# Turning the feed-forward's rounded values in fp32 instead of bf16, in a one-core transformer block

## The reference, cut to what matters

```
def act_quant(x):
    scale = 127.0 / jnp.clip(jnp.max(jnp.abs(x), axis=-1, keepdims=True), 1e-05)
    return jnp.clip(jnp.round(x * scale), -128, 127) / scale
...
h = bit_linear(x, w1)                      # 128 -> 512
h = depthwise_conv1d(h.transpose(0, 2, 1), conv_w, conv_b)
h = jax.nn.silu(h.transpose(0, 2, 1))
return bit_linear(h, w2)                   # act_quant(h), 512 -> 128, w2 in {-1, 0, 1} times a scale
```

## Time and profile before

| what | before |
|---|---|
| median of 3 runs | 264.71 us (264.69 to 265.05) |
| the profiled execution | 264.35 us |
| its span, first to last instruction | 262.4 us |
| TensorE busy | 254.0 us (97%) |
| VectorE busy | 217.1 us (83%) |
| ScalarE busy | 192.2 us (73%) |
| GpSimd busy | 31.1 us (12%) |

### The profile page before, as it was taken

The page is one execution under the profiler, slowest core; times in us unless marked ns, Lnnn a source line. Parts: engine busy times, 40 slices in busy tenths (PEclk is TensorE's granted clock), DMA queues, the critical chain, the costliest instruction groups (busy, mean ns, idle before and its releaser), DMA issues.

```text
span 262.4 us, 5607 instructions
## 1 busy us (share of the span) xinstructions
PE 254.0 (97%) x1869; PEld 189.2 (72%) x1869; DVE 217.1 (83%) x534; ACT 192.2 (73%) x463; POOL 31.1 (12%) x53
## 2 busy tenths in 40 slices
PE   7899999999999999999999999989999999999996
PEld 3568779779779878868787788767657565575675
DVE  5599979866766698998999787889899999899861
ACT  1689887788658678697899966179998699834551
POOL 3000002000000010201100102020003110424130
PEclk9999999999999999999999999999999999999999
DMA  6293491300400004300300000000000000000001
GB/s 184 56 239 97 95 343 32 90 4 0 95 1 1 2 0 101 86 0 4 92 4 0 0 2 0 4 0 1 2 0 4 4 1 0 2 9 4 21 10 40
DMA packets 8848, 10.70 MB, mean 41 GB/s; under 512 B 1115, under 2 KB 5877, under 8 KB 8821
## 3 DMA queue, kind: packets, MB, share of 16 engines
q1 hardware_dynamic: 7792, 9.70, 13.7%
q10 hardware_dynamic: 1029, 0.65, 0.8%
HBM read 4.99 MB, written 0.52 MB: 21 GB/s over the span
## 4 chain that ended last, share of the span: by engine, by line
PE 70%; DVE 18%; ACT 5%; issue 5%; POOL 1%; DVEq 0%; ACTq 0%; POOLq 0%
PE slot L518 19%; PE slot L608 13%; PE slot L589 6%; PE slot L590 6%; PE slot L564 3%; PE slot L615 3%; DVE mx L1152 3%; PE slot L570 2%; PE slot L761 2%; PE slot L755 2%; DVE RB L1157 2%; ACT S L910 2%; PE slot L706 2%; PE slot L749 2%; PE slot L579 2%
## 5 line engine op out<-in xcount | busy, mean ns | idle before, releaser
L1046 DVE TENSOR_REDUCE nm<-slot 128x1 f32<-128x589 f32 x64 | 47.6, 766 | 9.7 <-PE slot L590 9.3
L838 ACT ACTIVATE PR<-slot,nm 128x589 f32<-128x589 f32 x64 | 47.7, 749 | 9.3 <-DVE nm L1046 8.8
L518 PE MATMUL slot<-K,PR 128*128 128x128 f32 (+1 forms) x320 | 44.3, 276 | 0.2
L589 PE MATMUL slot<-KH,Q 128*128 128x296 f32 (+1 forms) x128 | 42.1, 345 | 0.2
L518 PEld LDWEIGHTS slot<-K,PR 128*128 128x128 f32 (+1 forms) x320 | 36.1, 142 | 8.1 <-ACT PR L838 5.0
L608 PE MATMUL slot<-PT,V 128*64 128x256 f32 (+1 forms) x320 | 38.1, 384 | 0.7 <-ACT PT L773 0.7
L773 ACT ACTIVATE PT<-slot 128x640 f32<-128x640 f32 x47 | 32.2, 705 | 8.3 <-PE slot L518 7.3
L590 PE MATMUL slot<-KL,Q 128*128 128x296 f32 (+1 forms) x128 | 36.1, 299 | 0.0
L910 ACT ACTIVATE S<-slot,mx 128x77 f32<-128x77 f32 x128 | 29.2, 365 | 6.3 <-DVE mx L1152 5.6
L608 PEld LDWEIGHTS slot<-PT,V 128*64 128x64 f32 (+1 forms) x320 | 22.1, 137 | 12.3 <-issue 3.5
L589 PEld LDWEIGHTS slot<-KH,Q 128*128 128x128 f32 x128 | 24.2, 189 | 3.6 <-issue 1.4
(11 more groups left out here) (169 smaller groups left out, 478.2 us busy)
## 6 DMA issues: line engine op xcount, KB each, us to landing
KH<-KH SPq DMA_DIRECT2D x16, 147.5 KB, 2.5
KL<-KL SPq DMA_DIRECT2D x16, 147.5 KB, 2.6
CTT<-in_ctxT SPq DMA_DIRECT2D x1, 640.0 KB, 3.9
K<-in_const SPq DMA_DIRECT2D x1, 589.0 KB, 4.9
WGU<-in_wgu SPq DMA_DIRECT2D x1, 580.0 KB, 6.0
out<-X SPq DMA_DIRECT2D x8, 64.0 KB, 1.5
L1W<-in_l1w SPq DMA_DIRECT2D x1, 384.0 KB, 3.8
WD<-in_wdT SPq DMA_DIRECT2D x1, 320.0 KB, 6.5
```

The costliest lines, as they stand in the source:

```text
L518: return pe.transpose(dst, src, ident[0:p, 0:p])
L589: pe.matmul(W[:, K0 + lo:K0 + hi], q, KH[:, g % 4, lo:hi], start=True, stop=False)
L838: act.activation(PR[:, s, :], W[:, K0:K0 + KEYS0], ACT.Exp, bias=nm0[:, s:s + 1], accum_out=sum0[:, b, p * 2 + f, t, e:e + 1]).then_inc(pr ...
L1046: dve.tensor_reduce(nm0[:, s:s + 1], W[:, K0:K0 + KEYS0], AX.X, ALU.max, negate=True).then_inc(max_ready, 1)
```

## The change

The stage f3 C, the buffers QB and identb and their semaphores go. f4 F turns QM itself in fp32, MAGIC still in it, once it is rounded; the turned tile fills a whole bank. f4 A1 takes MAGIC away while it converts to bf16. The result of f4 B goes to the start of the bank. f3 A1 of tile n now waits until f4 F of tile n - 2 is through.

```
                 elif kind == "f4":
                     n = upto(item)
-                    pe.wait_ge(*quantised(n))
-                    pe.wait_ge(identb_ready, 1)
-                    Wb = W[:, 0:256].bitcast(BF16)
+                    pe.wait_ge(rounded, n)
                     for c in range(HC):
-                        mm = pe.transpose(Wb[:, c * P:(c + 1) * P], QB[:, (n - 1) % 2, c * P:(c + 1) * P], identb[:])
+                        mm = turn(W[:, c * P:(c + 1) * P], QM[(n - 1) % 2][:, c * P:(c + 1) * P])
...
                     if n > 2:
-                        act.wait_ge(*quantised(n - 2))
+                        act.wait_ge(front_done, NTH[KINDS["f4"][n - 3]] + 1)
...
-                    act.activation(QBT[:, (n - 1) % 2, :], W[:, 0:256].bitcast(BF16), ACT.Copy).then_inc(qbt_ready, 1)
+                    act.activation(QBT[:, (n - 1) % 2, :], W[:, 0:HID], ACT.Copy, bias=-MAGIC).then_inc(qbt_ready, 1)
...
-                    dve.wait_ge(ld["ident"], 16)
-                    dve.tensor_copy(identb[:], ident).then_inc(identb_ready, 1)
```

```
-w:F4 n:P2 a2:F2+5@0 w:A1 a1:F3 n:D3 w:D1 a1:A1 a2:D1 o:F1 o:F0 a4:F2 o:D1 o:D1 a4:F0 n:P2 a2:F7 a1:P1 a4:D1 n:D3 a4:A1 f1:F6+18@5 f1:A1 a4:F4
-a4:D1 f1:D1 f2:F6 a4:B a2:D1 f2:F7 a1:P1 a4:A1 f2:A1 a4:D1 a4:B a4:Ca f2:A1 a4:Ca f2:F3 f2:D1 f2:A1 f2:F6+4@2 f2:A2 f2:D1 f2:D2 f2:A1 a4:A1 a4:F0
...
+a2:F4+5@0 w:D1 o:F7 o:F1 a2:D1 a4:F2 o:D1 o:D1 n:P2 a4:D1 a1:F6 a4:F0 a1:A1 a4:A1 a4:F4 a4:B+12@6 n:D3 a1:P1 a4:Ca f1:F6 a2:F3+4@7 a4:D1 f1:A1 a4:D1
+f1:D1 a4:A1 f2:F6 f2:A1 a2:D1 f2:F2 f2:A1 a4:B a4:Ca f2:D1 f2:D1 f2:F3 f2:A1 a4:A1 f2:D1 a4:F6 f2:A2 f2:F1 f2:A2 a4:B+5@0 f2:D2 f2:A1 f2:A2 a4:D1
...
-m2:A2 m2:D2 m4:F6 m2:P1 m2:D1 m2:D2 m4:D2 m4:B m4:A1 m4:F0 m4:A1 m4:B m4:B m4:D2 m4:D2 m4:D2
+m4:A1 m4:F2 m4:A1 m4:D2 m4:B m4:B+2@0 m4:D2 m4:D2
```

More of the change, by code:

```diff
@@ L107 @@
[L107 to L120, removed]
@@ L134 @@
[L134 to L137 removed]
+x0:F4 x0:A1 k:F0 q:F6 k:A1 q:A1 k:D1 k:F2 k:A1 q:D1 v:F4 v:F0 k:D1 u:F6 u:F2 v:Ca u:F4 v:Ca u:F0 u:D1 u:D1 u:A1 u:A1 u:B
@@ new lines @@
+u:D1 u:B u:A1 u:D1 u:Ca u:A1 u:B u:F6 u:B s:D2 u:Ca u:Cd u:D1 u:A1 u:F4 u:Ca u:D1 v:F2 u:A1 v:Ca s:F3 u:B s:D1 q:F0
+u:Ca w:D0 u:B u:F2 u:Ca u:D1 q:A1 u:A1 w:P1 k:F6 u:F4 q:D1 u:D1 k:A1 u:A1 w:F1 k:D1 u:B w:A1 u:B u:F6 w:D1 u:Ca u:Ca
+u:F2 u:D1 u:F0 u:D1 w:D0 u:F4 u:A1 u:B w:P1 u:A1 u:B u:D1 u:A1 u:Cd u:D1 u:B u:F6 u:D1 u:Ca u:Ca q:F3 u:A1 u:F0 q:A1
+u:A1 u:B w:F2 x0:D2 u:B u:D1 u:A1 u:Cd u:F4 q:D1 u:B w:D0 w:A1 w:D1 u:D1 u:Ca x0:P2 u:F6 u:A1 u:Ca w:P1 a3:F2 u:B u:F0
+u:D1 u:A1 u:B a3:D1 x0:D3 u:Ca u:Ca k:F4 u:F2 w:F7 k:A1 u:D1 u:D1 u:A1 u:B u:A1 u:Ca k:D1 g:F6 g:D1 w:A1 u:F4 u:B u:Ca
@@ new lines @@
+u:F0 u:D1 u:A1 w:D1 w:D0 q:F6 u:F2 u:D1 u:A1 u:B w:P1 u:Cd q:A1 w:F7 q:D1 w:A1 u:F4 u:B u:D1 w:D1 w:D0 u:A1 u:Ca u:D1
+u:F6 u:B u:F0 u:D1 u:A1 u:A1 u:B u:Cd u:Ca u:D1 u:A1 x0:F2 u:B a3:F4 u:Cd a3:D1 u:B u:F6 x0:A1 u:Ca w:P1 k:F2 k:A1 u:D1
+u:F0 w:F5 w:D0 u:D1 u:A1 u:B w:P1 w:A1 k:D1 w:D1 u:F2 u:F4 u:Ca u:A1 w:F7 u:D1 u:B u:D1 a3:P1 u:A1 u:A1 w:A1 u:B u:Ca
+u:B w:D1 w:D0 q:F6 u:Ca u:F0 q:A1 w:P1 u:Cd u:F4 w:F7 u:D1 u:A1 u:B u:D1 u:A1 u:F2 w:A1 q:D1 w:D1 u:D1 u:Ca o:F7 u:A1
+u:F0 u:B o:D1 u:B u:D1 u:Ca u:F6 u:Cd u:A1 w:D0 u:D1 u:F4 u:B u:Cd q:F3 q:A1 q:D1 w:P1 w:F2 u:D1 u:A1 w:A1 u:B w:D1
@@ new lines @@
+u:A1 u:F0 o:F2 u:Ca u:F6 u:D1 u:D1 u:B u:A1 u:A1 u:Cd u:B o:F3 u:Ca u:F4 o:D1 o:D1 n:P2 u:D1 u:B w:D0 v:F0 u:Ca u:A1
+w:P1 k:F2 v:Ca n:D3 k:A1 u:F6 u:B u:D1 k:D1 u:Ca v:F0 u:A1 u:F4 u:D1 u:B u:Cd v:Ca u:F2 k:F0 u:A1 u:B u:D1 u:A1 u:Cd
+o:F7 k:A1 u:B u:F4 k:D1 u:Ca o:D1 n:P2 v:F6 u:D1 u:F2 v:Ca u:A1 u:D1 w:F1 u:A1 w:A1 n:D3 u:B u:B u:Ca u:F6 f1:F0 u:D1
+u:F4 w:D1 u:Ca u:D1 q:F3 f1:A1 f1:D1 u:A1 u:B f2:F2 u:A1 u:B u:Cd u:F6 w:D0 q:A1 u:Ca q:D1 w:D0 u:D1 u:F0 w:P1 u:F4 u:D1
+f2:A1 u:A1 w:F3 u:D1 u:B f2:D1 u:A1 u:B u:A1 w:A1 u:B w:D1 u:Ca u:Cd f2:F6 u:F2 f2:F7 f2:A2 f2:D2 u:Ca f2:A1 u:F0 u:D1 k:F4
@@ new lines @@
+u:A1 f2:D1 f2:A1 k:A1 u:D1 u:B w:P1 u:A1 f2:D1 w:F6 k:D1 u:Ca w:A1 u:B f2:A2 u:Ca w:D0 w:D1 u:F2 u:F4 w:P1 f2:F7 f2:A2 f2:A1
+f2:D2 u:D1 u:F0 u:D1 f2:D1 w:F6 u:D1 u:A1 u:A1 f2:D2 f2:A2 u:B w:A1 u:B u:A1 f2:D2 w:D1 f3:F7 u:B u:Ca u:Ca u:F2 u:F4 f3:D1
+f3:F6 u:Ca u:D1 f3:A1 f3:F1 u:A1 q:F0 u:D1 u:B f3:D1 u:Cd u:A1 w:D0 f3:A1 u:B u:Ca u:F6 u:F2 f3:D1 w:P1 f4:F4 q:A1 f4:A1 q:D1
+w:F5 u:D1 f3:A1 u:A1 w:A1 u:F0 u:D1 u:B u:A1 f4:B w:D1 u:D1 u:Ca f4:D2 u:A1 u:B a3:P1 u:Ca f4:F5 w:D0 f4:A1 u:F6 u:B f3:F4
@@ L215, in mega_kernel @@
         ident, ones = K[:, K_ID:K_ID + P], K[:, K_ONE:K_ONE + P]
-        identb = sb("identb", [P, P], BF16)
         bnx = sb("bnx", [P, 4, NT, 6])
@@ L398, in col @@
             return COL[:, COLS.index(name):COLS.index(name) + 1]
-        def quantised(n):
-            item = KINDS["f3"][n - 1]
-            return qb_copied[COPIES[item]], copied(item, COPIES[item])
         def half_pair(item):
@@ L730, in back @@
                     for c in range(HC):
-                        mm = pe.matmul(W[:, 2 * P:2 * P + D], QBT[:, (n - 1) % 2, c * P:(c + 1) * P],
+                        mm = pe.matmul(W[:, 0:D], QBT[:, (n - 1) % 2, c * P:(c + 1) * P],
                                        W2Q[:, c * D:(c + 1) * D], start=(c == 0), stop=(c == HC - 1))
@@ L802, in copy_values @@
                 engine.tensor_copy(dst, slot(item)[0:rows, 0:n * 512]).then_inc(v_copied["DVE"], 1)
[L804 to L814, removed]
         @block.scalar
@@ L953, in copy @@
             def copy(item):
-                {"u": copy_turned, "a4": copy_turned1, "v": copy_values, "f3": copy_quantised}[item[0]](act, "ACT", item)
+                {"u": copy_turned, "a4": copy_turned1, "v": copy_values}[item[0]](act, "ACT", item)
             walk("ACT", {"A1": first, "A2": second, "C": copy})
@@ L1201, in second @@
                     dve.wait_ge(f_done, n)
-                    dve.scalar_tensor_tensor(out=X2[:, m, :], in0=W[:, 2 * P:2 * P + D], scalar=aq2[:, m, 3:4],
+                    dve.scalar_tensor_tensor(out=X2[:, m, :], in0=W[:, 0:D], scalar=aq2[:, m, 3:4],
                                              in1=X1[:, m, :], op0=ALU.mult, op1=ALU.add).then_inc(x2_ready, 1)
@@ L1286, in copy @@
             def copy(item):
-                {"u": copy_turned, "a4": copy_turned1, "v": copy_values, "f3": copy_quantised}[item[0]](dve, "DVE", item)
+                {"u": copy_turned, "a4": copy_turned1, "v": copy_values}[item[0]](dve, "DVE", item)
             walk("DVE", {"D0": early, "D1": first, "D2": second, "D3": third, "C": copy})
```

32 lines of the change are left out of this document (13 added, 19 removed).

## The result

| what | before | after |
|---|---|---|
| median, runs of one chip | 265.35 us (264.44 to 266.73, 20 runs) | 266.03 us (265.40 to 266.64, 20 runs) |
| ratio, with 95% interval | | 1.003 (1.0017 to 1.0043) |
| span of the profiled execution | 262.4 us | 264.6 us |
| TensorE, VectorE, ScalarE busy | 254.0, 217.1, 192.2 us | 253.7, 215.5, 191.1 us |

A forecast was written before the change was run, and what follows sets the result against it. TensorE was taken to bound 10 to 165 us, VectorE 165 to 247 us, then TensorE alternating with copies. Terms of +1.07 and -1.49 us gave -0.42 on 264.71: 264.3 us, called no change, range 263.1 to 266.0.

The forecast's parts named there:

- Part 1: Turns in fp32 on TensorE: before 165 us they cost +0.84 us in full, after it nothing.
- Part 4, the runs of u F: First stage, TensorE: new order has 49 runs of score matmuls instead of 44, +0.45 us.
- the two fillers gone: New order up to `w 1 3 1`: two fewer fillers on the bounding TensorE, -0.22 us.
- Part 2: Copies to bf16 dropped: after 165 us VectorE loses 1.28 us, gains a 0.82 us copy; net -0.46 us.
- Part 3: f3 A1's wait moves to f4 F of tile n - 2; already over when ScalarE arrives, 0 us.
- Part 4, the holes: Second stage: VectorE's two waits, at 174.76 and 187.40 us, close in the new order, -0.82 us.
- Part 4, the collision: Second stage: VectorE's L1169, slowed beside GpSimd's L506, may escape; half the 0.86 us taken, -0.43 us.
- Part 4, the last fillers: Kernel's end: two fillers ahead of the last m4 B on TensorE are not hidden, +0.22 us.
- Rival 2: Slower: feed-forward chain with ScalarE's exponentials sets the second stage, savings return as waits before f4 D2; 266.0 us, chance 0.19.
- Rival 3: With 26 fewer fillers TensorE's clock drops to 1.2 GHz in the second stage; about +5.8 us, 270.5 us, chance 0.05.

The follow-up runs named there:

- e8: The edit in the kernel before's old order, with four QM buffers instead of two; 265.47 us, 1.0004 of the kernel before.
- e10: Kernel before with two idle turns added ahead of each of the four f4 F of b = 0; 265.64 us, 1.0013.
- e7: Kernel before without any of its 85 fillers; 266.92 us, 1.0050.
- e17: Kernel before with the bf16 copies of the first two tiles of b = 1 on ScalarE instead of VectorE; 266.37 us, 1.0045.
- e11: Changed kernel with one second-attention copy moved from VectorE to ScalarE, ahead of the first f4 A1 of b = 1; 266.48 us, 1.0036 of the kernel before.
- e1: The code edit alone in the kernel before's order, only the f3 C stages gone; 267.79 us, 1.0096 of the kernel before.
- e9: Changed kernel with four QM buffers, in its own new order; 265.94 us, 1.0014 of the kernel before.
- e2: Code of the kernel before in the new order, each f3 C put back behind its f3 A1; 271.26 us, 1.0215.
- e6: Changed kernel without any of its 59 fillers; 268.13 us, 1.0104 of the kernel before.
- e12: Edit, old order, four QM buffers; second f4 F, first f4 B and one a4 F ahead of a6 F, four fillers dropped; 271.47 us, 1.0234 of kernel before.

## Why the prediction was wrong, step by step

Of the 1.7 us between the forecast of 264.3 and the measured 266.03, 0.64 are the kernel before itself: it has 265.35 in 20 runs, where I stood on 264.71 from three. The rest is the change, forecast at -0.4 and measured at +0.7 (+1.03 in the two traces).

- **Part 1, first stage, +0.84: mis-sized.** The turn costs what I read, four in 0.43 us in after as well (151.78 to 152.21). It arrived at 0.42 us (e8), 0.49 of 0.87 (e10). A TensorE shown busy 153.9 of 155 us wasn't a TensorE without slack: its busy time includes modelled ends.
- **Part 4, the runs of u F, +0.45: a misreading.** A score matmul right behind five turns starts 0.47 us after them, most other instructions 0.55:

```profile
144.68 0.71 PE L509 MATMUL slot<-K,PR 128*128 128x128 f32 x5
145.23 0.60 PE L509 MATMUL slot<-K,W 128*128 128x128 f32 x4
...
152.21 0.71 PE L509 MATMUL slot<-K,PR 128*128 128x128 f32 x5
152.68 0.38 PE L580 MATMUL slot<-KH,Q 128*128 128x296 f32 x1
```

  The first score matmul gives back ahead of itself the 0.08 that it takes behind the earlier trace rows. Five turns stand ahead of 41 of the 93 runs of the two kernels; 25 of these start 0.46 to 0.48 after them, 15 at 0.52 to 0.55 and one at 0.59, so most give it back in full. With the two fillers gone (0.22 us, as e7 measured) and 0.42 for part 1 the rule gives 147.77 for the first stage; measured were 147.62. This stage's error was -1.02 us. That the runs cost nothing is argued from these rows; no run changed their number alone.
- **Part 2, second stage, -0.46: failed, and it is the step that decides.** "VectorE sets this stage" was read from one window. Where the copies stood ScalarE is the fuller engine; VectorE's freed 1.28 us became 1.35 us of waits and the stage took 0.21 us more (e8), e17 shows the sign, and in the new order 0.82 us less on VectorE became 0.73 more of waiting (e11).
- **Part 3, 0: mis-sized if at all.** In the old order the wait costs 0.9% (e1 against e8), as large as all else in this case. The new order is built around it, as I had read. With four buffers the ratio falls from 1.003 to 1.0014, intervals that overlap; in the traces it is 0.06 us. e9's expectation, within 0.1% of 1.003, is missed by the median.
- **Part 4, the holes, -0.82: failed as a price.** Both closed; 1.38 us of new ones came. I took my first value where the bounds were 0 and -0.82, although nothing showed that VectorE's sum set the pace there.
- **Part 4, the collision, -0.43: -0.16.** Before, L1169 lost 0.86 and a pair L989 at 241.81 another 0.44, which I hadn't counted; after, 0.85 and 0.29. (A pair at 200.20 before and at 201.79 after loses 0.40 in both.) That the loss is whole or nothing was wrong: 0.29 is a part.
- **Part 4, the last fillers, +0.22: right**, 0.16 to 0.17.
- **The rivals.** Rival 2 names the mechanism, as far as the runs show it, and nearly the time: the stage doesn't give, because the chain of the four tiles with ScalarE's exponentials in it sets f4 D2, and the savings come back as waits in front of it. My argument against it, that VectorE's largest wait there was 0.42 us, was no argument: an engine that is nearly full beside the one that sets the pace shows no waits either. What it had wrong is the first stage, +0.05 instead of +1.07, and the second, which lost 0.98 where it had only the fillers' 0.22. So its 266.0 us beside the measured 266.03 is luck: errors of -1.02 and +0.76 us, and the 0.64 of the kernel before. Rival 3 didn't happen in after. But my argument against it didn't hold (e2, e6, e7, e12).

What stays open: which small waits absorb half of an addition in the first stage; and of the second stage's +0.98 us only 0.2 for the edit (e8), 0.17 for the last fillers and 0.33 for the hole at o D1 are placed, the last without a cause. Some 0.3 us are not.

## What to carry to other kernels

Cut a stage into windows as short as its passages before naming its bound, and ask it of the very microseconds in which the removed instruction stood; when two engines are both above 90%, the fuller one is the first suspect, and moving one instruction between them tells by sign. Look in the trace where the difference arises before you put it down to what you moved: in e11 it was 55 us away. Price an instruction in a queue by the distance to what stands ahead of it as well as behind it. When an edit moves a buffer's release to a later stage, try it in the old order with more buffers first: here that came out level within 0.5 us, and the new order, which saves the two buffers, cost some 0.3 to 0.5 us of its own.
